# Experts normalised pair by pair in their last pass, and a quantised block whose rounding moves to ScalarE

## The reference

```python
logits = xt @ wg                                  # 1024 x 8
probs = softmax(logits); idx = argmax(probs)      # one expert per token
gate = probs[idx]
expert_out = einsum('nh,eoh->neo', xt, W) + b     # all eight, 256 x 256 each
out = einsum('ne,neo->no', onehot(idx) * gate, expert_out)
x = layernorm(x + out)
```

```python
def act_quant(x):    s = 127 / max(max|x| per token, 1e-5); return clip(round(x * s), -128, 127) / s
def weight_quant(w): s = 1 / max(mean|w|, 1e-5);            return clip(round(w * s), -1, 1) / s
h = x * rsqrt(mean(x * x) + 1e-5) * w_norm
value, gate = split(act_quant(h) @ weight_quant(w_gv).T)    # 1024 wide each
u = value * silu(gate)
x = layernorm(x + (x + act_quant(u) @ weight_quant(w_out).T))
```

## Time and profile before

| | us |
|---|---|
| median of 3 runs | 2238.8 |
| lowest and highest | 2238.22 and 2242.87 |
| the profiled execution | 2239.59 |
| its span | 2237.9 |
| block 2 and its norm, from the logits to the last copy | 311.6 to 394.8 |
| the scan of block 4 | 482 to 596 |
| block 5, from the end of the norm ahead of it to its own norm's last copy | 615 to 721 |

### The profile page before, as it was taken

One profiled execution on the slowest core, in us unless ns is written; L12 is line 12 of the kernel. 1 busy time (PEld: TensorE's weight loads), 2 busy tenths in 40 slices (PEclk: granted clock), 3 DMA queues, 4 the chain that ended last, 5 costly groups with the idle time before them and its releaser, 6 DMA issues.

```text
span 2237.9 us, 28822 instructions
## 1 busy us (share of the span) xinstructions
PE 1830.7 (82%) x10282; PEld 1275.4 (57%) x10286; DVE 1347.8 (60%) x2540; ACT 895.9 (40%) x2119; POOL 312.7 (14%) x269
## 2 busy tenths in 40 slices
PE   7755769647636877799999978997999999999997
PEld 3523444414413455566667847885666776666665
DVE  5369966779888641666667217885666424555325
ACT  1445530355322125366666026462555314444100
POOL 2304520015401025121111000000000000000001
PEclk9975569855566989899999989998999999999988
DMA  4010020100010210000001020000001000002000
GB/s 121 8 38 1 0 66 0 64 0 1 1 47 1 40 50 2 15 15 14 14 14 62 1 87 1 1 1 3 12 9 48 9 12 13 14 11 65 1 1 19
DMA packets 25798, 49.23 MB, mean 22 GB/s; under 512 B 6450, under 2 KB 19659, under 8 KB 24148
## 3 DMA queue, kind: packets, MB, share of 16 engines
q1 hardware_dynamic: 24148, 45.81, 6.7%
q10 hardware_dynamic: 1552, 2.10, 0.4%
HBM read 42.46 MB, written 1.05 MB: 19 GB/s over the span
## 4 chain that ended last, share of the span: by engine, by line
PE 56%; DVE 26%; issue 8%; ACT 6%; POOL 2%; DMA 1%; ACTq 1%; DVEq 0%; POOLq 0%; PEldq 0%
PE banks L1289 7%; PE banks L1355 7%; DVE big L972 6%; PE banks L1322 6%; PE banks L1367 5%; DVE big L582 3%; PE banks L1347 3%; PE banks L2212 3%; PE banks L1614 3%; PE banks L2005 2%; PE banks L1984 2%; PE banks L481 2%; PE banks L494 2%; ACT big L2111 2%; PE banks L1309 1%
## 5 line engine op out<-in xcount | busy, mean ns | idle before, releaser
L1443 DVE COPY arena<-banks 128x512 f32<-128x512 f32 x196 | 135.3, 690 | 260.8 <-PE banks L1347 258.7
L1355 PE MATMUL banks<-arena,big 128*128 128x256 f32 x784 | 216.0, 398 | 9.0 <-DVE arena L1443 8.9
L1322 PE MATMUL banks<-big 128*128 128x256 f32 x784 | 209.2, 390 | 1.6 <-ACT big L1480 1.6
L1506 ACT ACTIVATE arena<-banks,arena 128x256 f32<-128x256 f32 x392 | 193.1, 501 | 8.4 <-DVE arena L1398 4.9
L1289 PE MATMUL banks<-x_feat,arena 128*128 128x512 f32 x392 | 176.4, 593 | 1.2 <-ACT big L1490 1.2
L1355 PEld LDWEIGHTS banks<-arena,big 128*128 128x128 f32 x784 | 138.5, 190 | 66.5 <-DVE arena L1443 52.9
L227 POOL TENSOR_TENSOR ln_rstd<-ln_var_eps,neg_half 128x2 f32<-128x2 f32 x48 | 37.5, 782 | 913.7 <-DVE ln_var_eps L207 913.7
L1322 PEld LDWEIGHTS banks<-big 128*128 128x128 f32 x784 | 134.4, 191 | 28.2 <-issue 14.5
L1398 DVE TENSOR_REDUCE arena<-banks 128x2 f32<-128x512 f32 x196 | 134.5, 686 | 24.7 <-PE banks L1322 24.5
L972 DVE TENSOR_TENSOR_SCAN big<-big,banks 128x1024 f32<-128x1024 f32 x64 | 145.7, 2279 | 0.0
L1090 POOL TENSOR_TENSOR big<-big,arena 128x1024 f32<-128x1024 f32 x64 | 128.6, 2009 | 103.5 <-DVE big L972 100.4
(11 more groups left out here) (310 smaller groups left out, 3307.2 us busy)
## 6 DMA issues: line engine op xcount, KB each, us to landing
arena<-in_L0f_w SPq DMA_DIRECT2D x1, 2048.0 KB, 8.2
arena<-in_L1a_wo SPq DMA_DIRECT2D x1, 2048.0 KB, 16.1
arena<-in_L1f_gv SPq DMA_DIRECT2D x1, 2048.0 KB
arena<-in_L2a_qk_w SPq DMA_DIRECT2D x1, 2048.0 KB
arena<-in_L2x_wo SPq DMA_DIRECT2D x1, 2048.0 KB, 7.4
arena<-in_L2x_q_w SPq DMA_DIRECT2D x16, 128.0 KB, 2.0
arena<-in_L2x_kv_w SPq DMA_DIRECT2D x16, 128.0 KB, 2.0
arena<-in_L2f_up SPq DMA_DIRECT2D x1, 2048.0 KB
```

The source lines that it names most:

```text
L1322: last = mm(ps[:, h * SEQ:(h + 1) * SEQ], q[:, b * SEQ + h * P:b * SEQ + (h + 1) * P], k[:, b * SEQ:(b + 1) * SEQ], start=not self.mask, s ...
L1355: last = mm(slot, self.v[:, 2 * b + kc, :], self.probs_t[:, u % 2, kc, :], start=(kc == 0), stop=(kc == 1))
L1443: v.tensor_copy(self.probs_t[:, u % 2].rearrange("p a b -> p (a b)"), B[4 + u % 2][:]).then_inc(self.turn_read, 1)
L1506: last = a(self.probs[:, u % 2, h, :], B[2 + u % 2][:, h * SEQ:(h + 1) * SEQ], ACT.Exp, bias=self.neg_max[:, u % 2, h:h + 1], scale=scale, ...
```

## The change

In block 2 VectorE frees the banks at once, so the first pass of experts waits for no coefficient. The coefficients are transposed within the first pass, the biases are multiplied and added behind it, two passes run in the loop, and the last pass is written out with the layer norm's steps between its tiles.

In block 5 the weights' absolute sums (4 passes of 1024 columns) and their scaling and rounding (12 passes of 1024 columns) go to ScalarE, one pass in each of 16 of the scan's steps. The means are made in step 12 of the scan: TensorE multiplies once with the lane sums and four times with the absolute sums, into bank 4, and VectorE reads the results. Only one clipping pass for each weight stays in block 5. The token norm takes the variance that the layer norm has made instead of new squares. The copies of the transposed tokens go to ScalarE. In the loop over tiles the two rounding passes go to ScalarE, which runs them behind the next tile's two sigmoids, and one small product goes to GpSimd, transposing runs one tile and the output two tiles behind, and the layer norm's steps run between the tiles. The zero matmuls and `add_up` are gone.

```diff
 class TopExpert:
+        self.after = LayerNorm(e, l, turn_bank=lambda pair: pair)
     def tensor(self, pe):
-        with pe.Fori(0, EXPERTS // 2) as i:
-            for t in range(TILES):
-                pe.wait_ge(self.expert_read, TILES * i + t + 1)
...
-        pe.wait_ge(self.coef_ready, 1)
...
+        for t in range(TILES):
+            expert(0, t)
+            if t in (3, 5):
+                half = t // 5
+                pe.wait_ge(*((self.coef_t_ready, 1) if half else (self.coef_ready, 1)))
+                for k in range(4):
+                    last = nc.tensor.transpose(B[1][0:EXPERTS, k * P:(k + 1) * P], self.coef[:, 4 * half + k, :], e.ident[:])
+                last.then_inc(self.coef_t_psum, 1)
         pe.wait_ge(self.coef_t_ready, 2)
         for t in range(TILES):
             last = mm(e.y_bank(t), self.coef_t[:, t * P:(t + 1) * P], self.bias, start=True, stop=True)
...
+        with pe.Fori(0, EXPERTS // 2 - 2) as i:
+            for t in range(TILES):
+                expert(i + 1, t)
+        for t in range(TILES):
+            expert(EXPERTS // 2 - 1, t)
+            if t in (5, 7):
+                self.after.turn(pe, (t - 5) // 2)
+        for pair in (2, 3):
+            self.after.turn(pe, pair)
     def vector(self, dve):
+        dve.sem_inc(self.expert_read, 4)
...
-        dve.sem_inc(self.expert_read, 4)
...
+        for t in range(TILES):
+            add(last, t)
+            if t % 2:
+                dve.wait_ge(self.expert_read, TILES * last + t + 5)
+                self.after.moments(dve, t // 2)
+                if t > 1:
+                    self.after.normalise(dve, t // 2 - 1)
+        self.after.normalise(dve, TILES // 2 - 1)
 class StateSpace:
     def scalar_slot(self, act, s):
         if s + 1 < STEPS:
             self.scalar_step(act, s + 1)
+        if self.guest:
+            self.guest.scalar_weights(act, s)
     def tensor_slot(self, pe, s):
+        if self.guest and s == self.guest.MEANS:
+            self.guest.tensor_means(pe, self)
     def vector_slot(self, dve, s):
+        if self.guest and s == self.guest.MEANS:
+            self.guest.vector_means(dve)
 class BitLinear:
+    ABS, MEANS, ROUNDS = 6, 12, 15
+    def scalar_weights(self, act, s):
...
+        if self.ABS <= s < self.ABS + 4:
+            k = s - self.ABS
+            a(self.absolute, gv[:, k * n:(k + 1) * n], ACT.Abs, accum_out=self.abs_sum[:, k:k + 1]).then_inc(self.abs_ready, 1)
+            act.wait_ge(self.abs_ready, k + 1)
+        if self.ROUNDS <= s < self.ROUNDS + 12:
+            k, second = divmod(s - self.ROUNDS, 2)
...
+            if second:
+                act.wait_ge(self.rounded, 2 * k + 1)
+                a(piece, piece, ACT.Identity, bias=e.rounds[:, 1:2]).then_inc(self.rounded, 1)
+            else:
+                act.wait_ge(self.inv_ready, 1)
+                a(piece, piece, ACT.Identity, bias=e.rounds[:, 0:1], scale=self.w_inv[:, k // 4:k // 4 + 1]).then_inc(self.rounded, 1)
+    def tensor_means(self, pe, scan):
+        pe.wait_ge(scan.s_driven, self.MEANS + 1)
...
+        pe.wait_ge(self.means_read, 2)
     def tensor(self, pe):
...
         for t in range(TILES):
+            hidden(t)
+            if t >= 1:
+                turn(t - 1)
+            if t >= 2:
+                down(t - 2)
+            if t in (5, 7):
+                self.after.turn(pe, (t - 5) // 2)
+        turn(TILES - 1)
+        down(TILES - 2)
         down(TILES - 1)
...
-        for pair in range(4):
-            mm(B[pair][:], e.ident_bf[:], self.zero, start=True, stop=True).then_inc(e.y_ready, 1)
+        for pair in (2, 3):
+            self.after.turn(pe, pair)
     def vector(self, dve):
-        v.tensor_reduce(self.abs_sum[:, 0:1], flat(self.gv_f), AX.X, ALU.add, apply_absolute_value=True).then_inc(self.abs_ready, 1)
-        dve.wait_ge(self.means, 1)
...
+        e.wait_x_tok(dve, self.l)
+        ch.link(dve, v.tensor_tensor(self.ms, e.ln_mean_var[:, :, 1], e.ln_rstd[:], ALU.mult))
+        ch.link(dve, v.tensor_tensor(self.ms, self.ms, e.ln_rstd[:], ALU.mult))
+        v.tensor_scalar(self.ms, self.ms, EPS, None, ALU.add).then_inc(self.x_norm_in, 1)
+        dve.wait_ge(self.rounded, 12)
+        v.tensor_scalar(flat(self.gv_q), flat(self.gv_f), 1.0, -1.0, ALU.min, ALU.max).then_inc(self.gv_clipped, 1)
         dve.wait_ge(self.rooted, 1)
...
         def output(t):
             dve.wait_ge(self.out_psum, t + 1)
+            dve.wait_ge(self.h_inverse, t + 1)
             v.scalar_tensor_tensor(e.x_tok[:, t, :], B[5][:, 0:D], self.h_inv[:, t:t + 1], e.x_tok[:, t, :], ALU.mult, ALU.add).then_inc(self.out_read, 1)
+            if t % 2:
+                dve.wait_ge(self.out_read, t + 1)
+                self.after.moments(dve, t // 2)
...
-            self.quantise(dve, ch, self.hid_q[t % 2], self.hid[:, t, :], self.h_scale[:, t:t + 1]).then_inc(self.hid_q_ready, 1)
-            if t:
-                output(t - 1)
+            if t >= 2:
+                output(t - 2)
+            if t in (5, 7):
+                self.after.normalise(dve, (t - 5) // 2)
     def scalar(self, act):
...
-            if t:
-                self.turn(act, t - 1)
+            if t >= 1:
+                self.quantise_hidden(act, t - 1)
+            if t >= 2:
+                self.turn(act, t - 2)
+            if t == 7:
+                self.after.keep(act, 0)
+    def quantise_hidden(self, act, t):
+        act.wait_ge(self.h_scaled, t + 1)
+        e.act_chain.link(act, a(self.hid[:, t, :], self.hid[:, t, :], ACT.Identity, bias=e.rounds[:, 0:1], scale=self.h_scale[:, t:t + 1]))
+        a(self.hid_q[t % 2], self.hid[:, t, :], ACT.Identity, bias=e.rounds[:, 1:2]).then_inc(self.hid_q_ready, 1)
```

More of the change, by code:

```diff
@@ L752, in __init__ @@
         self.e, self.l, self.name = e, l, name
-        self.hosted = room is not None
+        self.hosted, self.guest = room is not None, None
         a, big = arena, e.big
@@ L1670, in scalar @@
             nc.scalar.activation(self.coef_t[:, half * BANK:(half + 1) * BANK], e.bank[1][0:EXPERTS, :], ACT.Copy).then_inc(self.coef_t_ready, 1)
+        self.lanes.add(act)
+        self.after.scalar(act)
     def gpsimd(self, pool):
-        pass
+        self.after.gpsimd(pool)
 HIDDEN = 1024
@@ new lines, in tensor_means @@
+    def tensor_means(self, pe, scan):
+        e, mm = self.e, self.e.nc.tensor.matmul
+        pe.wait_ge(scan.s_driven, self.MEANS + 1)
+        for k in range(4):
+            if k == 0:
+                e.wait_set(pe, self.l)
+                pe.wait_ge(e.lanes_summed, 1)
+                mm(e.bank[4][:, 1:2], e.ones[0:LANES, :], e.lane_sums[:, 0:1], start=True, stop=True)
+                pe.wait_ge(self.abs_ready, 4)
+            last = mm(e.bank[4][:, 0:1], e.ones[:], self.abs_sum[:, k:k + 1], start=(k == 0), stop=(k == 3))
+        last.then_inc(self.means, 1)
+        pe.wait_ge(self.means_read, 2)
@@ new lines, in vector_means @@
+    def vector_means(self, dve):
+        e, v, ch = self.e, self.e.nc.vector, self.e.dve_chain
+        e.wait_set(dve, self.l)
+        ch.link(dve, v.memset(self.w_inv, 1.0))
+        dve.wait_ge(self.means, 1)
+        for k, w in enumerate((self.gv_f, self.out_f)):
+            size = w.shape[1] * w.shape[2] * P
+            v.tensor_scalar(self.w_mean[:, k:k + 1], e.bank[4][:, k:k + 1], 1.0 / size, EPS, ALU.mult, ALU.max).then_inc(self.means_read, 1)
+        dve.wait_ge(self.means_read, 2)
+        v.reciprocal(self.w_inv, self.w_mean).then_inc(self.inv_ready, 1)
@@ L1765, in tensor, with hidden, turn @@
             last.then_inc(self.x_t_psum, 1)
-        def down(t):
+        def hidden(t):
+            for q in (2, 3, 0, 1):
+                if t:
+                    pe.wait_ge(self.hid_done, 2 * t - 1 + q % 2)
+                for c in range(CH):
+                    last = mm(B[q][:], self.x_q_t[:, c, t * P:(t + 1) * P], self.gv_q[:, c, q * BANK:(q + 1) * BANK], start=(c == 0), stop=(c == CH - 1))
+                last.then_inc(self.gv_psum, 1)
+        def turn(t):
             pe.wait_ge(self.hid_q_ready, t + 1)
@@ L1893, in gpsimd @@
         self.e.nc.gpsimd.tensor_tensor(self.rs, self.ms, self.e.neg_half[:, 0:TILES], ALU.pow).then_inc(self.rooted, 1)
+        for t in range(TILES):
+            pool.wait_ge(self.h_maxed, t + 1)
+            self.e.nc.gpsimd.tensor_scalar(self.h_inv[:, t:t + 1], self.h_max[:, t:t + 1], 1 / QMAX, self.w_mean[:, 1:2], ALU.mult, ALU.mult).then_inc(self.h_inverse, 1)
+            if t >= 3 and t % 2:
+                self.after.root(pool, (t - 3) // 2)
+        self.e.wait_set(pool, self.l + 1)
+        self.after.root(pool, 3)
 PK_HEADS, PK_TOP, PK_KEYS, PK_DIM, PK_EXPERTS = 4, 8, 128, 64, 2048
@@ L2476, in build @@
             scans = which in (1, 4)
-            if which >= 10:
+            if which == 5:
+                next(b for m, b in blocks if m == 4).guest = blocks[-1][1]
+            if which in (2, 5) or which >= 10:
                 continue
```

143 lines of the change are left out of this document (72 added, 71 removed).

## The result

The changed kernel took 2217.49 us (median of 4, 2210.66 to 2220.97) against 2238.51 for the kernel before (median of 4): the ratio is 0.9903, with a 95% interval of 0.9884 to 0.9923. Its profiled execution took 2216.6 us, with a span of 2214.9. The prediction was 2216.3, and the range 2207 to 2225. A second timing of the same kernel beside the experiments gave 2212.84 against 2235.05, a ratio of 0.9900 [0.9885, 0.9915].

What follows compares the result with a forecast made beforehand. TensorE bounds block 2, VectorE the scan, block 5's start and the tile loop. -6.7 + 1.9 - 16.1 - 1.6 = -22.5 us takes 2239.59 to 2217.1; the median, 0.8 lower, is 2216.3, range 2207 to 2225.

Steps and rivals of the forecast that it cites:

- Experts: Block 2: no wait for VectorE and the layer norm inside the last pass, -6.7 us, bounds -5.5 to -9.3.
- the 4.5 us of the working: Block 2: what bias matmuls (3.4 to 3.6) and coefficient transposes (some 1.0) cost TensorE in the expert stream.
- Scan: Scan: ScalarE's added passes are hidden, the means in step 12 are not: +1.9 us once, bounds +1.4 to +2.8.
- rival of longer passes: Scan and tile loop: ScalarE passes longer than 1.15 us, costing the scan above 1.59; 2248.8 us at 2.5; chance 0.04.
- Start of block 5: From last normalise to the norm product: L1831 at 618.0 instead of 634.07, -16.1 us, bounds -15.0 to -16.5.
- the longer of GpSimd's 1.64 and the clipping pass: Start of block 5: power and 2.29 us clipping pass run side by side, so only the longer counts.
- Loop and tail: Block 5's tile loop and what follows tile 7: 72.6 us against 74.2, -1.6 us.
- the clock's two levels: Tile loop and tail: 64.9 us (-9.3) with TensorE at full clock, 80.3 (+6.1) at half.
- the ring: Tile loop: sigmoids, rounding, copy, transposes, output and next tile's matmuls wait in a circle, 6.6 to 8.6 us a tile.
- the turn: Tile loop, t = 5: TensorE waits for VectorE's normalise before turning the norm's first pair, 3.4 us more.
- half-clock rival: Tile loop: TensorE stays at half clock, 2224.0 us; chance 0.19.
- the +4.8: Tile loop: if moving the rounding to ScalarE cost 6.4 us, the -1.6 would become +4.8, the sum -16.1.

Runs made afterwards that it cites:

- lagged kernel: Changed kernel with transposes and output matmuls one tile later and the first pair's turn behind tile 6: 2200.66 us, 0.9846 of the kernel before.
- later turn: Changed kernel with TensorE's turn of the layer norm's first pair behind tile 6 instead of tile 5: 2205.53 us, 0.9870 of the kernel before.
- block5_only: Kernel before with only the quantised block and its guest work in the scan changed, experts as before: 2220.37 us, ratio 0.9942.
- after: The whole change against the kernel before, first timing and profile: 2217.49 us, ratio 0.9903.
- warm_gap: Changed kernel with eighteen unread matmuls on TensorE ahead of L840 in the scan's preparation: 2211.34 us, 0.9896 of the kernel before.
- after_again: The changed kernel unedited, timed a second time beside the experiments: 2212.84 us, 0.9900 of the kernel before.

## Why the prediction came out

**Experts: right in size, in part by luck.** -6.60 us against -6.7. Biases and transposes cost the 4.5 us of the working. But the first root, which the working had 61.5 us behind the logits, came 62.7 us behind them: the 3.4 us at half clock behind the biases were in no term, and by an estimate from their length and the two levels they are worth 1.7. What brought the clock down there was not tested. The lost time came back because the later pairs were 3.74 apart instead of 4.1, and because 2.08 us instead of 2.54 passed from the last normalise to the end of the last copy.

**Scan: right, the means a little dear.** +1.60 and +1.54 against +1.9; reads and handover took less. Steps stayed at 3.52 with one pass in each. The rival of longer passes was priced too high: the run with two passes puts the point where they begin to cost at about 3.52 - 0.47 - 1.22 = 1.83 us of ScalarE time from start to start, with the lead on top, not at 1.59.

**Start of block 5: the term was mis-sized by 1.4 us.** -14.68 against -16.1. The step that failed is "the longer of GpSimd's 1.64 and the clipping pass": side by side they took nearly as long as one after the other. Clip and power together took 3.78 us, from 610.34 to 614.12, and 2.29 + 1.64 is 3.93; the clip moved away brought the 1.64 back. The Trainium skill, "SBUF — State Buffer", section "Who interferes with whom", says that VectorE and GpSimd share a pair of ports, that a tensor_scalar on VectorE can take it for the whole instruction, and that the engine that comes second then blocks fully. The trace agrees: the power, issued 0.17 us behind the pass, ended 1.49 us after it and took 3.61, and 1.64 where no pass stood beside it.

**Loop and tail: the mechanism was right, the size is within the clock.** -1.1 in the first profile, +1.3 in the second, against -1.6, with -9.3 and +6.1 for the clock's two levels. Tile 7 came 51.7 us behind the first hidden matmul (51.8 in the working), and the tail took 21.1 us (20.8). That the ring sets it, and that the turn costs 3.4 us, the lagged kernel and the later turn show. The half-clock rival did not come true, though the clock fell to 0.73 in the tiles and 0.66 in the tail (0.65 in the tiles of the second profile): TensorE kept switching between the two levels, as the outputs of 1.04 and 1.91 us show. The working took the first tile's start from the edge of its window, 646.7; it was 647.15, so the loop and tail before took 73.88 us and not 74.2. The price of a ScalarE pass is not what decides, for with rounding on VectorE the loop took as long; the +4.8 that the prediction worked out beside the rule of the Trainium skill, "ScalarE: Activation LUTs", section "Rules for kernel authors", came in neither profile. The Trainium skill, "Perfetto Trace Analysis", section "Optimizing Scalar/DVE Operations", says that handing work to ScalarE can pay where VectorE is saturated; with the ring open that was 11.9 us.

**What was not in the sum.** The preparation of the scan took 2.3 us longer, for TensorE's clock, in a stretch for which the working had no row. With it the changed stretch should have gained 22.5 - 2.3 - 1.4 - 0.5 + 0.3 = 18.6, which is what the first profile shows. The medians say about 21.7, with an interval of 17 to 26. The 3 us between them lie in code that was not changed, whose length scatters by 15 us over the profiles. Most of that is TensorE's clock in block 6, which took 198.9 us at a granted clock of 0.955 (block5_only) and 210.4 at 0.889 (after). In the first pair of profiles the rest is 4.4 us shorter: 2.5 of them lie ahead of the logits, block 6 is 1.5 longer, and the stretch from block 9's last copy to block 10's 3.3 shorter (the others add up to 0.2). That stretch took 391.2 us in both profiles with the experts of before and 388.0 in eleven of the twelve with the new ones (384.9 in warm_gap), with one stretch of 6.8 us at the lower clock less. So the median met the forecast closer than its terms did, and part of that is luck; whether the change has a share in the rest of the span, in that stretch above all, stays open.

**The rivals.** No table was loaded inside the loop. The change did what it says, and the weights were in time.

## What to carry to other kernels

Work that is moved from a bound engine to idle time of another can be worth nearly its whole length, but look next for the ring that the new order closes: here 14.7 us at the start of block 5 came at once, for 1.6 in the scan, and 14 to 16 more lay in a ring of waits over ScalarE and TensorE that one tile of lag and a later turn opened. Where somebody waits for a GpSimd operation, look what VectorE does beside it: here a clipping pass in another place was worth 1.97 us. And compare kernels by stretches with the granted clock beside them, before a difference of a few microseconds in the whole is given a cause.

## What the runs showed of the hardware that was not expected

- GpSimd's power on 128x8 took 3.61 us beside a VectorE pass of 4096 columns and 1.64 alone, in kernels that differ only in where the clipping passes stand and where in SBUF they write.
- Nine matmuls without a use, 7.89 us in an idle gap, made the stretch behind them 3.0 us shorter, because L840 then ran in 3.68 instead of 6.72 us.
- The same unedited code met TensorE's clock in two patterns: block 3 and the preparation took 39.7 and 50.1 us in some profiles and 40.9 and 47.8 in others, and the clock's rises had parted by 2 us before the first edited instruction of the experts.
- ScalarE's operations, three times in a row of four, followed one another about 0.1 us sooner than their durations say: two passes of 1.14 us and 1.92 of other work took 3.91 us.
- The table load ahead of the first sigmoid ran while ScalarE still waited for the hidden matmuls, so the first sigmoid came 0.86 us behind the first of them (1.26 in after_again), not 2.03 as before.
